# Down products with w2's high and low part side by side, in a routed feed-forward block

## The reference, cut to what matters

```python
gates = zeros((T, e)).at[arange(T)[:, None], top_i].add(top_p)      # T = 2048, e = 4, two experts a token
h = silu(einsum('td,edf->etf', xf, w1)) * einsum('td,edf->etf', xf, w3)   # d = 256, f = 1024
expert_out = einsum('etf,efd->etd', h, w2)
out = einsum('te,etd->td', gates, expert_out)
x = x + tanh(g_ffn[0]) * out
```

## Time and profile before

| what | value |
|---|---|
| median of 3 runs | 512.54 us (511.25 to 513.44) |
| the profiled execution | 516.16 us, span in the profile 514.2 us |
| TensorE busy (matmul) | 485.6 us, 94% |
| VectorE busy | 400.4 us, 78% |
| ScalarE busy | 316.7 us, 62% |
| GpSimd busy | 188.1 us, 37% |
| full slots (L1782, L1802) | from 177 to 470 us of the span |
| half-tile slots (L1831, L1842) | from 467 to 503 us |

### The profile page before, as it was taken

The page is one execution under the profiler, slowest core; times in us unless marked ns, Lnnn a source line. Parts: engine busy times, 40 slices in busy tenths (PEclk is TensorE's granted clock), DMA queues, the critical chain, the costliest instruction groups (busy, mean ns, idle before and its releaser), DMA issues.

```text
span 514.2 us, 11413 instructions
## 1 busy us (share of the span) xinstructions
PE 485.6 (94%) x3622; PEld 443.5 (86%) x3622; DVE 400.4 (78%) x940; ACT 316.7 (62%) x759; POOL 188.1 (37%) x191
## 2 busy tenths in 40 slices
PE   9889999999888999999999999999999999999991
PEld 7557777777666899999999999999999999999880
DVE  2687898898997588888688888888878788887550
ACT  3224457556433766587577676677767777777760
POOL 2524656448765305263035263112202220222111
PEclk9996999999987999999999999999999999999996
DMA  8999885000211311323112232022212111211110
GB/s 269 355 388 395 358 314 206 21 22 12 74 43 48 119 31 38 62 43 60 26 18 43 70 65 42 23 42 31 33 24 42 21 30 22 31 22 23 20 12 10
DMA packets 32392, 45.13 MB, mean 88 GB/s; under 512 B 9709, under 2 KB 28781, under 8 KB 32109
## 3 DMA queue, kind: packets, MB, share of 16 engines
q1 hardware_dynamic: 24807, 34.66, 19.9%
q0 software_dynamic: 6576, 8.92, 10.5%
q10 hardware_dynamic: 960, 0.94, 0.6%
HBM read 33.50 MB, written 21.82 MB: 108 GB/s over the span
## 4 chain that ended last, share of the span: by engine, by line
PE 68%; DVE 17%; issue 5%; POOL 4%; ACT 3%; ACTq 1%; DVEq 0%; POOLq 0%
PE ps_scores L1782 21%; PE ps_wide L1802 7%; PE ps_probT L1782 7%; PE ps_misc L1802 7%; PE ps_wide L1607 5%; DVE w_lo L1413 3%; PE ps_misc L1629 3%; PE ps_scores L1578 2%; PE ps_scores L1831 2%; DVE w_lo L1409 2%; PE ps_misc L1552 1%; POOL score L1100 1%; DVE lowest L1267 1%; PE ps_probT L1588 1%; PE ps_wide L1842 1%
## 5 line engine op out<-in xcount | busy, mean ns | idle before, releaser
L1176 POOL DMA_INDIRECT out_x<-y_out,meta x35 | 63.6, 1817 | 194.5 <-ACT y_out L974 189.4
L1413 DVE TENSOR_TENSOR w_lo<-w,w_hi 128x512 fp32r<-128x512 f32 x152 | 104.3, 686 | 16.1 <-ACT w_hi L931 8.3
L1782 PE MATMUL ps_scores<-xt_hi,w_hi 128*128 128x256 f32 x384 | 110.9, 289 | 0.2 <-DVE xt_lo L1427 0.2
L1782 PE MATMUL ps_scores<-xt_lo,w_hi 128*128 128x256 f32 x384 | 108.8, 283 | 0.0
L1782 PE MATMUL ps_scores<-xt_hi,w_lo 128*128 128x256 f32 x384 | 108.8, 283 | 0.0
L931 ACT CAST w_hi<-w 128x512 fp32r x152 | 95.5, 629 | 4.7 <-issue 4.3
L1782 PEld LDWEIGHTS ps_scores<-xt_hi,w_hi 128*128 128x128 f32 x384 | 73.7, 192 | 0.4 <-DVE xt_lo L1427 0.4
L1782 PEld LDWEIGHTS ps_scores<-xt_lo,w_hi 128*128 128x128 f32 x384 | 73.8, 192 | 0.0
L1782 PEld LDWEIGHTS ps_scores<-xt_hi,w_lo 128*128 128x128 f32 x384 | 73.7, 192 | 0.0
L945 ACT ACTIVATE act_g<-ps_scores 128x256 f32<-128x256 f32 (+1 forms) x114 | 42.3, 371 | 36.7 <-PE ps_scores L1782 23.2
L1100 POOL TENSOR_TENSOR score<-score,lowest 128x616 f32<-128x616 f32 x32 | 38.9, 1215 | 52.5 <-DVE lowest L1267 52.1
(11 more groups left out here) (237 smaller groups left out, 1233.1 us busy)
## 6 DMA issues: line engine op xcount, KB each, us to landing
grouped<-in_pad SPq DMA_DIRECT2D x1, 10296.0 KB
w<-in_L_ffn_w SPq DMA_DIRECT2D x8, 1024.0 KB, 12.5
w2s<-in_L_ffn_w SPq DMA_DIRECT2D x4, 1024.0 KB, 13.6
xg<-grouped SPq DMA_DIRECT2D x16, 256.0 KB, 2.7
out_x<-xall SPq DMA_DIRECT2D x8, 256.0 KB
xall<-in_x SPq DMA_DIRECT2D x1, 1024.0 KB, 13.1
xall<-in_x SPq DMA_DIRECT2D x1, 768.0 KB, 7.3
ctxT<-in_ctx_t SPq DMA_DIRECT2D x2, 308.0 KB, 5.0
```

The source lines that it names most:

```text
L1176: pool.indirect_dma_start(out, bass.IndirectOffsetOnAxis(ap=meta[:, s % 2, t, E:E + 1].bitcast(U32), axis=0), y_out[:, s % 2, t, :], None, ...
L1413: dve.tensor_tensor(w_lo[:, f % NB], unit_weights(e, f), w_hi[:, f % NB].bitcast(F32), ALU.subtract).then_inc(w_lo_done, 1)
L1782: mm = pe.matmul(ps_gu[f % NB][:, m, 0:n], lhs, rhs[:, a, c, 0:n], start=(k == 0), stop=(k % (3 * DC) == 3 * DC - 1), skip_group_check=True)
```

## The change

`w2_hi` and `w2_lo` become two halves of one buffer, `w2_both`, so that high and low part of a unit lie side by side as 512 columns. In a full slot `down` issues per tile one matmul of 512 moving columns (hidden high x both parts) and one of 256 (hidden low x w2 high) instead of three of 256. A tile now has a whole bank, `ps_y[t]`, whatever the parity of the slot: the first half collects what is multiplied by w2 high, the second what is multiplied by w2 low. ScalarE's `scale` multiplies the first half by the gate and counts up a new semaphore, `y_begun`. A new VectorE instruction per tile, `scale_low`, multiplies the second half by the gate, adds `y_out` and counts up `y_scaled`; it stands in unit 1 of the next slot, behind `weights_lo`. VectorE gets a second `expert_of` at the start of a slot. On TensorE `down` of unit 0 moves from behind `up` of unit 2 to behind `up` of unit 3, followed there by `down` of unit 1; and it waits for `y_scaled` of the slot just before. The half-tile slots keep their products; their first down product now waits for the last full slot's `y_scaled` too.

```diff
-        w2_hi = sb("w2_hi", [P, 2, 2, D], F32R)
-        w2_lo = sb("w2_lo", [P, 2, 2, D], F32R)
+        w2_both = sb("w2_both", [P, 2, 2, 2, D], F32R)
+        w2_hi, w2_lo = (w2_both[:, :, :, i] for i in range(2))
...
-                        act.activation(y_out[:, a, t], ps_y[a][:, t], ACT.Copy, scale=gate_of).then_inc(y_scaled, 1)
+                        if tiles_of(s) == TH:
+                            act.activation(y_out[:, a, t], ps_y[t][:, 0], ACT.Copy, scale=gate_of).then_inc(y_begun, 1)
+                        else:
+                            act.activation(y_out[:, a, t], ps_y[a][:, 0], ACT.Copy, scale=gate_of).then_inc(y_scaled, 1)
...
+                def scale_low(s, a, e):
+                    for t in range(TH):
+                        dve.wait_ge(y_begun, TH * s + t + 1)
+                        dve.scalar_tensor_tensor(out=y_out[:, a, t], in0=ps_y[t][:, 1], scalar=meta[:, a, t, bass.ds(e, 1)], in1=y_out[:, a, t],
+                                                 op0=ALU.mult, op1=ALU.add).then_inc(y_scaled, 1)
...
+                    if not first:
+                        e_before = expert_of(dve, s - 1)
                     e = expert_of(dve, s)
...
+                        if f == 1 and not first:
+                            scale_low(s - 1, 1 - a, e_before)
...
-                    if f == 0 and is_slot(s, 1):
+                    if f == 0 and is_slot(s, 0):
                         pe.wait_ge(x2_done, B)
-                    if f == 0 and not (isinstance(s, int) and s < 2):
-                        pe.wait_ge(y_scaled, tiles_before(s - 1))
+                    if f == 0 and not is_slot(s, 0):
+                        pe.wait_ge(y_scaled, tiles_before(s))
...
-                        wh, wl = (w[:, f // 2 % 2, f % 2] for w in (w2_hi, w2_lo))
-                        for i, (lhs, w) in enumerate(((hh, wh), (hh, wl), (hl, wh))):
-                            mm = pe.matmul(ps_y[a][:, t], lhs, w, start=(f == 0 and t == 0 and i == 0),
-                                           stop=(f == FC - 1 and i == 2), skip_group_check=True)
+                        both = w2_both[:, f // 2 % 2, f % 2]
+                        pe.matmul(ps_y[t], hh, both, start=(f == 0), stop=(f == FC - 1), skip_group_check=True)
+                        mm = pe.matmul(ps_y[t][:, 0], hl, both[:, 0], start=False, stop=(f == FC - 1), skip_group_check=True)
...
-                        if f >= 2:
+                        if f == 3:
+                            down(s, 0, a)
+                        if f >= 3:
                             down(s, f - 2, a)
-                        elif not is_slot(s, 0):
+                        elif f < 2 and not is_slot(s, 0):
                             down(s - 1, FC - 2 + f, 1 - a)
...
-                        pe.wait_ge(y_scaled, tiles_before(s - 1))
+                        pe.wait_ge(y_scaled, tiles_before(max(s - 1, FULLS)))
```

More of the change, by code:

```diff
@@ L676, in flamingo_block @@
         up_done, silu_done, hid_done, hid_hi_done, hid_lo_done = sem("up_done"), sem("silu_done"), sem("hid_done"), sem("hid_hi_done"), sem("hid_lo_done")
-        down_done, y_scaled = sem("down_done"), sem("y_scaled")
+        down_done, y_begun, y_scaled = sem("down_done"), sem("y_begun"), sem("y_scaled")
         inner_turned, inner_copied = sem("inner_turned"), sem("inner_copied")
@@ L1427, in x_lo @@
                     dve.tensor_tensor(xt_lo[:, a, :, 0:n], ps_x[:, :, 0:n], xt_hi[:, a, :, 0:n].bitcast(F32), ALU.subtract).then_inc(x_lo_done, 1)
+                def scale_low(s, a, e):
[3 more added lines that the diff above has]
+                                                 op0=ALU.mult, op1=ALU.add).then_inc(y_scaled, 1)
                 def slot(s, a):
-                    last, n = is_slot(s, SLOTS - 1), tiles_of(s) * P
+                    first, last, n = is_slot(s, 0), is_slot(s, SLOTS - 1), tiles_of(s) * P
+                    if not first:
+                        e_before = expert_of(dve, s - 1)
                     e = expert_of(dve, s)
@@ L1454, in short @@
                     last = s == SLOTS - 1
+                    if s == FULLS:
+                        e_before = expert_of(dve, s - 1)
                     e = expert_of(dve, s)
@@ L1464, in short @@
                             weights_lo(u + AHEAD, e_after, f + AHEAD - FC)
+                        if f == 1 and s == FULLS:
+                            scale_low(s - 1, 1 - a, e_before)
                         if f == 5 and not last:
```

## The result

The changed kernel takes 527.38 us (median of 4 runs, 523.64 to 528.99) against 512.0 for the kernel before (4 runs): ratio 1.0269, 95% interval 1.0233 to 1.0304. By the ratio it is some 13.8 us slower, by the two medians 15.4. Forecast were 524.6 us within 517 to 531, that is 12.1 us slower.

A forecast was written before the change was run, and what follows sets the result against it. TensorE's stream was taken to bound the full slots. Stalls and added VectorE work, net of savings, summed as 1.7 + 3.9 + 2.3 + 0.9 + 2.2 + 1.1 = 12.1 us on 512.5: 524.6 us, range 517 to 531.

The forecast's parts named there:

- The saving of TensorE: In `down` of full slots, 0.335 us replaces 0.360 per tile: 0.025 saved, 0.40 a slot, 6.4 us in all.
- Rival D: In `down`, 512 columns cost two times 256, so TensorE saves nothing: 2 us more than (A), 527 us; chance 7%.
- (A): The forecast itself: in every slot TensorE stalls for longer than it saves; chance 75%.
- Rival E: 512 columns take 0.131 us, so VectorE and ScalarE set the pace of the full slots: 518 us; chance 3%.
- The loop: Full slots such as 12 and 13: stall 0.73 and 1.17 us, less 0.40 saved, net +0.33 and +0.77.
- lag: Time from TensorE's start of `up` of unit 2 to VectorE's `weights_lo` of unit 1; predicted stall: lag - 0.90 us.
- Slots 3, 8 and 9: Slot 3 was forecast like slot 12 at +0.33 us, slots 8 and 9 like slot 13 at +0.77 each.
- slots 4 and 6: Slots with routing: stall 1.85 us with 0.5 carried for the second load, net 1.45, less 0.3 relief: +1.15 each.
- The half-tile slots: The first `short_down` waits until VectorE has freed the banks at 472.18 instead of starting at 471.05: +1.1 us.
- The low end: Lower bound of the forecast time: -7.6 us when several open terms meet, giving 517 us.
- Rival B: No stall comes, as VectorE's `scale_low` ends before `up` of unit 3: faster, 506 us; chance 6%.
- Rival C: Lags shrink after each stall and loads cost nothing, so stalls about equal savings: 512 to 515 us; chance 9%.

The follow-up runs named there:

- e2: Changed kernel without VectorE's `scale_low` and its second register load, ScalarE's `scale` releasing the banks: ratio 1.0009 to the kernel before.
- e1: Changed kernel with the 512-column `down` matmul split into two of 256 columns: 527.28 us, ratio 1.0280 to the kernel before.
- e7: Kernel before with the third `down` matmul of each tile cut to 128 columns: one run, slots of 17.42 us against 17.71.
- e11: Kernel before with only VectorE's second register load added at the start of a slot, its value unused: ratio 1.0036.
- e4: Changed kernel without VectorE's second register load, `scale_low` using the present slot's gate: ratio 1.0210 to the kernel before.
- e5: Kernel before with VectorE's part added (second register load, multiply-add per tile), banks still alternating: ratio 1.0123.

## Why the prediction was right

It named the outcome and its mechanism, a stall of TensorE once a slot on the banks that VectorE's new instruction releases. By its own steps:

**The saving of TensorE** failed: 6.4 us were forecast, 0.025 a tile. Measured are 0.006 a tile (e2), 1.6 us in all, and nothing that can be told by the time (e1). The step that failed is that "the weight load that goes with each matmul is the only thing left" to explain 0.120 us for 256 columns, and with it the price of 0.215 for 512. That figure of the earlier trace rows belongs to plain fp32 passes of 256 columns; 512 fp32r columns take 0.235. Against the 0.12 of 256 columns, the further 256 cost (0.235 - 0.12) / 256 = 0.45 ns each. So 256 columns need 0.115 by themselves, about as long as a load (0.118 in e7). Rival D, 512 columns at twice 256, had 7% and said 527 us, which is what was measured; its mechanism, the stall of (A) without the saving, is the nearest to what happened. That the forecast hardly suffered is due to what the prediction said of the term under D: a saving before the wait is eaten by the wait, all but 0.16 us a slot.

**The 131 ns of the Trainium skill** ("TensorE: Matmul & The Clock Gate", section "Back-to-back issue gap") are not what this kernel gets: its rows have 0.235 us for load and matmul of 512 fp32r columns. Rival E is refuted.

**The loop.** Slot 12 was forecast at +0.33 and took +0.35 (18.06 less 17.71); slot 13 at +0.77 and took +0.83 (18.54). The agreement is in part luck, for inside errors cancelled: the saving was 0.10 in place of 0.40 and the stall 0.45 in place of 0.73. The stall was smaller because TensorE came to the bank 0.06 earlier and not 0.24, and because nothing of the second load was carried to it, where the prediction had 0.2. In slot 12 the lag is 1.65 with nothing but the load added (e11), 1.64 with the load and no merged matmul (e1), 1.70 in the changed kernel and 1.71 in it without the load (e4). So the 0.07 by which it exceeds the 1.63 of before comes from TensorE's saving and not from the load. The new instruction was 0.48 us against 0.45.

**Slots 3, 8 and 9** were put into the classes of slots 12 and 13 without reading their lags. The timeline of before has 1.18, 2.79 and 2.20 us there, that of the changed kernel 1.06, 1.76 and 1.71, and they took -0.08, +0.38 and +0.36 against +0.33, +0.77 and +0.77: 1.2 us less than forecast.

**Slots 0 to 8** were forecast at +6.8 and took +8.1. Slots 1 and 2 came as forecast (2.2 and 2.14 together). The mis-sized terms are slots 4 and 6, 1.15 each against 2.17: the lag grew by 1.04 us in slot 4 and by 0.94 in slot 6, where 0.5 was carried for the second load, and no relief of 0.3 is seen in them. In slot 4 the load is nearly all of it (idle 0.48 to 1.46, lag 2.51 without it). In slot 6 it is 0.42; the rest stays without the load (lag 3.05 in e4, 2.53 before). I also set the wait of `up` of unit 3 at nothing outside slots 1 and 7, where slots 4 and 6 have it as well; as I read it, that wait is no cost of its own: in slot 4 VectorE frees the bank 4.96 us after the start of `up` of unit 2, TensorE has 2.88 us to do until then, and it stands for the rest, before `up` of unit 3 or before `down`. The cause was also put too narrowly: I took VectorE as the pace only in slots 1 and 2; e5 shows its work costing time in slots 4 to 7 without any new wait. These 2.0 us too little and the 1.2 too much of slots 3, 8 and 9 cancelled in part, which is luck again.

**The half-tile slots** were forecast at +1.1; the wait is 1.2. With slot 15 the forecast from there to the end is +1.9, and +2.2 were measured.

**The low end** of the range does not follow quite: the four open terms that are listed add up to 7.1, not 7.6. Nothing hangs on it.

**Rival B**, no stall, is refuted by the waits. **Rival C**, lags that shrink until stalls about equal savings, is refuted too. Lags did shrink in slots 3, 5 and 7 to 9, most in slot 8 (2.79 to 1.76), and the load did cost nothing in the loop. But in slots 10, 12 and 14 the lag stayed (1.70 against 1.63 in slot 12), and in every slot from 1 on but slot 3 the stall was well above the saving, in the loop at least four times.

## What to carry to other kernels

Before fewer, wider matmuls are built, time one of the wide shape in the same data type: at 0.45 ns a column a merge saves nothing once the columns take as long as the weight load. When accumulators stop alternating, the release of a bank becomes a race between the path that frees it and what the matmul engine has left to do; put the lag of the freeing engine, read at one of its instructions, against that amount, and read it in every slot, not in one of each kind. If the lag is larger, moving the first consumer later works until the next thing needed (here the weights of the next unit) is as late, and two such moves can spend one slack twice.

## What the runs showed of the hardware that was not expected

At granted clock 1.00 a matmul of 512 fp32r columns takes 0.235 us from start to start, one of 256 0.12, one of 128 0.06; but the one behind 128 columns takes 0.18, and the loads of 128x128 weights keep starting 0.12 us apart in that stream (e7). A second register load from SBUF on VectorE put off the next instruction by 0.32 us behind an instruction of 0.68 us (slot 12), and nothing of that shows in the time of the loop (e11, e4). Behind short routing instructions it added 0.98 us of idle time in slot 4 of the changed kernel and 0.62 in slot 6. What makes the difference is not shown: the load alone, in the kernel before, added 0.63 in slot 4 (e11).
